# A transformer block on one core: the adapter attention joined to the first maxima in 16 turns, a tail that begins with the third tile's products, and weight splits of 512 columns

## The reference, cut to what matters

```python
mod = (silu(c) @ wmod).reshape(1, 6, 1, C); sa, ca, ga, sb, cb, gb = ...
h = layernorm(x) * (1 + ca) + sa
q, k, v = split(h @ w_attn.T)                 # 32 heads of 32, q and k rotated
y = softmax(causal(q @ k.T / sqrt(32))) @ v
ak, av = split(adapter_wte @ w_attn.T)[1:]    # 10 rows
y = y + gating[0] * softmax(q @ ak.T / sqrt(1024)) @ av
x = x + ga * (y @ w_proj.T)
h = layernorm(x) * (1 + cb) + sb
x = x + gb * top2_mixture_of_experts(h, gate_w, expert_w)
```

## Time and profile before

| | |
|---|---|
| median of 3 runs | 2748.28 us |
| the profiled execution | 2752.79 us, span 2751.0 us |
| granted TensorE clock, mean | 0.948 of full speed |
| busy share | PE 91%, DVE 60%, POOL 48%, ACT 38% |
| `front` | 0 to 680 us |
| `adapter_attention` | 680 to 809 us |
| `attention` up to the main loop's first exponential | 809 to 880 us |
| main loop and first two tiles | 880 to 2010 us |
| `tail`: projections and routing | 2010 to 2290 us |
| `tail`: experts | 2290 to 2751 us |

### The profile page before, as it was taken

The page is one execution under the profiler, slowest core; times in us unless marked ns, Lnnn a source line. Parts: engine busy times, 40 slices in busy tenths (PEclk is TensorE's granted clock), DMA queues, the critical chain, the costliest instruction groups (busy, mean ns, idle before and its releaser), DMA issues. The chain is left out here.

```text
span 2751.0 us, 40043 instructions
## 1 busy us (share of the span) xinstructions
PE 2493.5 (91%) x13407; PEld 1626.6 (59%) x13407; DVE 1657.0 (60%) x3261; ACT 1048.0 (38%) x1877; POOL 1308.5 (48%) x827
## 2 busy tenths in 40 slices
PE   6789999998758999999999999999859875999997
PEld 4667677776534444444444444444348764888885
DVE  5544555110558777777777777777526554777775
ACT  3521011111331555555555555555501111444443
POOL 4452342000432767676767666667724443333232
PEclk9999999999886999999999999999979987999998
DMA  7356655212743515151515151512356754878885
GB/s 262 108 161 192 176 167 169 93 39 63 261 131 78 134 37 134 38 133 40 131 40 132 40 127 40 120 48 55 106 190 214 162 122 175 307 284 292 306 288 179
DMA packets 231903, 397.21 MB, mean 144 GB/s; under 512 B 44540, under 2 KB 95292, under 8 KB 231620
## 3 DMA queue, kind: packets, MB, share of 16 engines
q1 hardware_dynamic: 204340, 319.62, 40.2%
q0 software_dynamic: 17152, 50.38, 5.3%
q10 hardware_dynamic: 10256, 25.21, 2.9%
HBM read 299.22 MB, written 103.76 MB: 146 GB/s over the span
## 5 line engine op out<-in xcount | busy, mean ns | idle before, releaser
L1227 ACT ACTIVATE t_prob<-t_scores_psum 128x512 f32<-128x512 f32 (+3 forms) x1280 | 610.5, 538 | 449.2 <-PE t_scores_psum L1102 242.4
L1355 POOL TENSOR_TENSOR t_two<-t_prob 128x1024 f32<-128x1024 f32 (+1 forms) x321 | 694.4, 2184 | 166.5 <-ACT t_prob L1227 103.2
L1255 DVE TENSOR_REDUCE t_part<-t_seen_psum 128x1 f32<-128x512 f32 x768 | 479.5, 683 | 146.4 <-PE t_seen_psum L1075 142.3
L1075 PE MATMUL t_seen_psum<-t_k_stack,t_q_stack 97*128 97x512 f32 (+3 forms) x1283 | 523.4, 420 | 40.1 <-DVE t_q_stack L1243 22.5
L1098 PE MATMUL t_scores_psum<-t_q_stack,t_k_stack 98*128 98x512 f32 (+3 forms) x1280 | 504.2, 405 | 8.7 <-ACT t_prob L1227 7.4
L1098 PEld LDWEIGHTS t_scores_psum<-t_q_stack,t_k_stack 98*128 98x128 f32 x1280 | 243.0, 191 | 307.8 <-ACT t_prob L1227 172.5
L1075 PEld LDWEIGHTS t_seen_psum<-t_k_stack,t_q_stack 97*128 97x128 f32 x1283 | 257.5, 201 | 92.3 <-DVE t_part L1255 37.1
L1261 DVE CUSTOM_DVE_ANT_0 t_seen_psum<-t_seen_psum,t_causal 128x128 f32<-128x128 f32 (+3 forms) x515 | 250.7, 505 | 100.5 <-PE t_seen_psum L1075 90.2
L1116 PE MATMUL t_y_acc_psum<-t_prob,t_v 128*32 128x512 f32 (+3 forms) x2576 | 302.7, 542 | 0.0
L1630 PE MATMUL acc_psum<-z_e_hi,z_x_hi 128*128 128x512 f32 x576 | 228.4, 397 | 0.0
L1632 PE MATMUL acc_psum<-z_e_hi,z_x_lo 128*128 128x512 f32 x576 | 225.4, 391 | 0.0
(11 more groups left out here) (240 smaller groups left out, 3834.0 us busy)
## 6 DMA issues: line engine op xcount, KB each, us to landing
z_raw<-in_expert_w SPq DMA_DIRECT2D x80, 512.0 KB, 5.7
z_spare<-in_expert_w SPq DMA_DIRECT2D x72, 512.0 KB, 6.0
f_w_raw<-in_wmod SPq DMA_DIRECT2D x8, 2048.0 KB, 10.3
t_q_stack<-scratch_q_hi SPq DMA_DIRECT2D x64, 256.0 KB, 4.9
t_k_stack<-scratch_k_hi SPq DMA_DIRECT2D x64, 256.0 KB, 5.2
f_w_raw<-in_w_attn SPq DMA_DIRECT2D x24, 512.0 KB, 6.1
t_inverse<-scratch_inverse SPq DMA_DIRECT2D x132, 64.0 KB, 2.0
t_y<-scratch_a_y SPq DMA_DIRECT2D x33, 256.0 KB, 4.6
```

The source lines that it names most:

```text
L1075: nc.tensor.matmul(seen[:, n % BANKS, 0:width], q_stack[par][0:SEEN, h, t0:t0 + P], k_stack[par][0:SEEN, h, c * CH:c * CH + width], start= ...
L1227: nc.scalar.activation(prob[:, step % RING, h, c0:CH], scores[:, score_bank(step, h), c0:CH], ACT.Exp, scale=1.0 / math.sqrt(D)).then_inc( ...
L1255: nc.vector.tensor_reduce(dst, seen[:, n % BANKS], AX.X, ALU.max).then_inc(seen_free, 1)
L1355: nc.gpsimd.tensor_tensor(two[:, pair % 2, heads, c0:CH], a, b, ALU.add).then_inc(two_ready, 1)
```

## The change

The separate program for the adapter goes. Its work moves into the head of `attention`, in 16 turns of 1024 tokens of one group, and the 78 first entries of `order` are dealt out over the turns, half a share twice in a turn. `ak` and `av` stay where `front` left them, the buffers of the turns lie in the space of the second stacks and of v. The scores have 40 columns instead of 128 (8 products a turn), the spread of the weights goes from DVE to POOL (now with the inverse alone, the gating being multiplied into `av` once), the four memsets on POOL are put between turns, and the two on DVE go, since the stack of q loses its row of zeros (`see` has 96 rows instead of 97, `score` 97 instead of 98). The weight split begins at step 44, a piece of 512 columns every two steps, the copy on ACT and the difference on DVE. The tail loads ga first, DVE waits for ga alone, and PE's first work is the product of tile 2.

```diff
-def adapter_attention(nc, sem, consts, ak, av, q_hi_d, q_lo_d, out):
...
-        P_FROM, P_EVERY = STEPS - 20, 2
+        P_FROM, P_EVERY = STEPS // 2 + Y_LAG + 2, 2
...
-            c, at = divmod(step - lag - P_FROM, P_EVERY)
-            return c if i == G // 2 - 1 and at == 0 and 0 <= c < KC else None
+            piece, at = divmod(step - lag - P_FROM, P_EVERY)
+            return divmod(piece, 2) if i == G // 2 - 1 and at == 0 and 0 <= piece < 2 * KC else (None, 0)
...
+        def head_share(t, half):
+
+            at = [HEAD * x // (2 * TURNS) for x in (2 * t + half, 2 * t + half + 1)]
+            return range(*at) if t < TURNS else range(0)
...
+            def load_pair(t):
+                g, col = a_group(t)
+                if t >= 2:
+                    sp.wait_ge(a_q_ready, t - 1)
+                for src, dst in zip(q_parts, a_parts):
+                    sp.dma_start(dst[:, t % 2], src[g, :, col]).then_inc(a_loaded_q[t % 2], 16)
...
+            load_pair(0)
+            load_quarter(0)
...
+            for t in range(TURNS):
+                if t + 1 < TURNS:
+                    load_pair(t + 1)
+                if 1 <= t + 1 < NQ:
+                    load_quarter(t + 1)
+                if t == NQ:
+                    sp.dma_start(v[0][:, :, :], v_d[0]).then_inc(first_loaded[NQ], 16)
...
+            def a_score(t):
+
+                g = a_group(t)[0]
+                pe.wait_ge(a_q_ready, t + 1)
+                if t >= 2:
+                    pe.wait_ge(a_shifted, t - 1)
+                for j in range(2 * TPC):
+                    last = nc.tensor.matmul(a_scores(t)[:, j * HG * A:(j + 1) * HG * A], a_q[:, t % 2, j * P:(j + 1) * P],
+                                            ak[:, g].rearrange("p (h a) -> p h a", a=D)[:, :, 0:A], start=True, stop=True)
+                last.then_inc(a_scores_ready, 1)
...
+            def a_multiply(t, x):
+                pe.wait_ge(a_turn_ready, t + 1)
+                if (t, x) == (0, 0):
+                    pe.wait_ge(a_gated, 1)
+                else:
+                    pe.wait_ge(a_y_ready, 2 * t + x)
+                nc.tensor.matmul(y_acc[:, :], av[:, a_group(t)[0]], a_turn[:, t % 2, x * CH:(x + 1) * CH],
+                                 start=True, stop=True).then_inc(a_acc_ready, 1)
...
+            for t in range(TURNS + 2):
+                if t < TURNS:
+                    a_score(t)
+                head(t, 0)
+                if t >= 2:
+                    a_multiply(t - 2, 0)
+                    a_multiply(t - 2, 1)
+                head(t, 1)
+                if 1 <= t <= TURNS:
+                    if t == 1:
+                        pe.wait_ge(consts_loaded, 64)
+                    a_turn_over(t - 1)
...
+            pe.wait_ge(one_rows_set, 2)
             pe.wait_ge(sums_set, 2)
...
+            for t in range(TURNS + 2):
+                if t < TURNS:
+                    a_exp(t)
+                if t >= 2:
+                    a_keep_y(t - 2, 0)
+                    a_keep_y(t - 2, 1)
+                    a_store(t - 2)
+                if 1 <= t <= TURNS:
+                    a_keep_turned(t - 1)
...
+                    c, o = chunk_at(i, step, 3)
+                    if c is not None:
+                        act.wait_ge(p_loaded[c % 2], 16 * (c // 2 + 1))
+                        nc.scalar.activation(half_of(p_hi[:, c], o), half_of(p_raw[c % 2], o), ACT.Copy).then_inc(p_hi_done, 1)
...
-            for n in range(HEAD):
-                advance(0, n)
...
+            for t in range(TURNS):
+                if t > 0:
+                    dve.wait_ge(a_shifted, t)
+                a_shift(t)
+                head(t, 0)
+                if t > 0:
+                    dve.wait_ge(a_inv_ready, t)
+                a_norm(t)
+                head(t, 1)
...
-                        nc.vector.tensor_copy(p_hi[:, c], p_raw[c % 2]).then_inc(p_hi_done, 1)
-                        dve.wait_ge(p_hi_done, c + 1)
-                        nc.vector.tensor_tensor(p_lo[:, c], p_raw[c % 2], p_hi[:, c], ALU.subtract).then_inc(p_lo_done, 1)
+                        dve.wait_ge(p_hi_done, 2 * c + o + 1)
+                        nc.vector.tensor_tensor(half_of(p_lo[:, c], o), half_of(p_raw[c % 2], o), half_of(p_hi[:, c], o), ALU.subtract).then_inc(p_lo_done, 1)
...
+            for t in range(TURNS):
+                a_spread(t)
+                if t + 2 < TURNS:
+                    a_add(t + 2)
+                if t == 4:
+                    one_row(0, t)
+                if t == 7:
+                    nc.gpsimd.memset(prob[:, :, :, :], 1.0).then_inc(sums_set, 1)
+                if t == 10:
+                    nc.gpsimd.memset(two[:, :, :, :], 1.0).then_inc(sums_set, 1)
+            pool.wait_ge(a_scores_ready, TURNS)
+            one_row(1, TURNS - 1)
...
-        CONSTS = 16 * 8
+        CONSTS = 16 * 7
...
+            load_row(ga, 2, ga_loaded)
             load_y(EARLY)
             load_x(0)
+            load_row(scale_b, 4, consts_loaded)
+            load_row(shift_b, 3, consts_loaded)
             load_y(EARLY + 1)
...
             for n in range(EARLY, NT + LAG):
+                if n == EARLY:
+                    project(n)
                 if n == LAG:
                     pe.wait_ge(consts_loaded, CONSTS)
                     pe.wait_ge(made, 1)
                 if n >= LAG:
                     turn(n - LAG)
-                if n < NT:
+                if EARLY < n < NT:
                     project(n)
...
-            dve.wait_ge(consts_loaded, CONSTS)
+            dve.wait_ge(ga_loaded, 16)
```

More of the change, by code:

```diff
@@ L840, in attention @@
         p_hi, p_lo = p_parts
+        with ExitStack() as inner:
+            ab = lambda name, shape: inner.enter_context(nc.sbuf_tensor(f"a_{name}", shape, F32))
+            ab("filler", [P, 2 * HG * T])
+            a_y, a_turn = ab("y", [P, 2, 2 * CH]), ab("turn", [P, 2, 2 * CH])
+            a_prob, a_weight = ab("prob", [P, 2, 2 * CH]), ab("weight", [P, 2, AM, A])
+            a_top, a_total, a_inv = ab("top", [P, AM]), ab("total", [P, AM]), ab("inv", [P, 2, AM])
+            a_q, a_parts = ab("q", [P, 2, 2 * CH]), [ab(f"q_{n}", [P, 2, 2 * CH]) for n in ("hi", "lo")]
         q_stack, k_stack = [None, None], [None, None]
@@ L1031, in fetch @@
                 par, g = (1, ds(i * 2 + 1)) if half == 0 else (0, ds((i * 2 + 2) % G))
+                if (i, half, c, part) == (0, 0, 0, 0):
+                    for b in range(2):
+                        sp.wait_ge(a_stored[b], 16 * (TURNS // 2))
+                    sp.wait_ge(a_acc_ready, 2 * TURNS)
                 if (c, part) == (0, 0):
@@ new lines, in head @@
+            def head(t, half):
+                for n in head_share(t, half):
+                    if order[n][0] == "see" and order[n][3:] == (0, 0, 0):
+                        pe.wait_ge(first_loaded[order[n][2]], LOADS - 16)
+                    advance(0, n)
+            for t in range(TURNS + 2):
[8 more added lines that the diff above has]
+                    if t == 1:
+                        pe.wait_ge(consts_loaded, 64)
+                    a_turn_over(t - 1)
```

301 lines of the change are left out of this document (117 added, 184 removed).

## The result

The changed kernel takes 2727.61 us (median of 5, 2724.83 to 2730.89) beside 2751.15 us of before; the ratio is 0.990, 95% interval 0.9883 to 0.9916. It is faster by some 24 us, where I had forecast 67. The sign was right; the size was not, and 2727.6 lies above the range that I gave (2655 to 2720).

| part | marks in the traces | before | after | measured | forecast |
|---|---|---|---|---|---|
| A, joint stage | main loop's first exponential | 879.5 | 851.9 | −27.7 | −51 |
| main loop | from there to the 28th store of y's high part | 944.0 | 943.1 | −0.9 | 0 |
| B, weight split | 28th to 33rd (last) of these stores | 175.2 | 190.4 | +15.2 | −3 |
| C, tail | last store to the end | 752.3 | 740.3 | −12.0 | −13 |

What follows compares the result with a forecast made beforehand. PE was taken to bound nearly everything, except around 780 us and at the tail's start. From the median 2748.3 us, −51 −3 −13 = −67 gave 2681 us, own range 2660 to 2700, stated range 2655 to 2720.

Steps and rivals of the forecast that it cites:

- A: Joint stage of adapter and head: main loop's first exponential at 828.4 us, −51 us (−40 to −62).
- B: Weight split: copies go to ACT, half of the differences to steps 48 to 63; −3 us (−7 to +3).
- C: Tail: ga loads first and tile 2's product fills PE's wait; −13 us (−8 to −18).
- What bounds the kernel: PE nearly everywhere, except around 780 us and the tail's start; DMA, memsets and DVE pace stretches before the main loop.
- a turn at 6.6 us: Joint stage: PE's work and waits for 1024 tokens sum to 6.7, rounded to 6.6 us (6.2 to 7.6).
- the hand-off: Within a joint-stage turn: the second `av` product waits for ACT's copy of the shared PSUM tile, about 0.8 us.
- ten further turns at 6.6: Joint stage: after turn 5 at 744 us, ten turns bring the last scores to 810 us.
- the start: Joint stage's first turns: scores stand behind loads, coming near 690, 701, 712, 724 and 737 us, turn 5 at 744.
- memsets absorbed: Joint stage: slack of 3.2 us and a turn of lag absorb POOL's 6.92 us memsets, within a few us.
- The clock rival: Joint stage: PE's clock stays at its lower level, 12.9 us a turn, first exponential +17, total 2749 us; chance 0.10.
- The DMA rival: Joint stage: DMA bounds all of it, 157 us, first exponential at 858, total 2711 us; chance 0.09.
- No overlap: Joint stage: turns do not overlap, 16 us each, first exponential at 949, total 2802 us; chance 0.04.

Runs made afterwards that it cites:

- e7: The kernel of e2 with the second product of a turn in another bank than the first; 2695.8 us, ratio to before 0.981.
- e2: The changed kernel with the head's two rows of negative maxima issued by SP behind all loads of the turns; 2700.9 us, ratio to before 0.982.
- e12: The changed kernel with the split's 16 differences replaced by one-input multiplications by 1.0 on DVE; 2725.3 us, ratio to before 0.989.
- The seven traces: Traces of the changed kernel and six follow-up runs with the same joint stage; first exponentials between 846.9 and 864.7 us.
- e8: The kernel of e2 with the loads of the first group's quarters spread over the turns; 2691.3 us, ratio to before 0.980.
- e5: The changed kernel with the early weight split in pieces of 1024 columns every four steps, 8 differences instead of 16; 2717.7 us, ratio to before 0.988.
- e6: The changed kernel with the split's 512-column pieces one in each step from the last 20 steps on; 2717.6 us, ratio to before 0.987.
- e1: The changed kernel with the weight split as it was before the change; 2711.2 us, ratio to before 0.986.

## Why the prediction was wrong, step by step

- **What bounds the kernel**: right. PE's holes were where the page had them, and they were what could be gained. (Of slices 11 to 13 I wrote "5 and 9"; they read 7, 5 and 8. The 46.8 us are all of DVE's work, not its plain reductions alone. Neither enters the sum.)
- **A, where it went**: the first exponential came 23.5 us later than the forecast 828.4. The start has 7.6 of them (turn 5 at 751.6 instead of 744), the ten further turns 15.0 (81.0 instead of 66), the end 0.9.
- **A, a turn at 6.6 us**: right for an undisturbed turn, 6.2 to 6.7, with the hand-off at 0.8 to 0.9; e7 takes it away and has turns of 5.5. Scores 1.9, products 1.0 each, turned blocks 1.0. The last memset was covered by the last products, and the end took 19.3 us, as in the sum (18 to 19).
- **A, "ten further turns at 6.6"**: the step that failed, by omission. I listed what each moved step puts on PE, DVE, ACT and POOL and wrote that PE takes its entries in order, but not that SP does too: `load_row` waits for `minus_ready`, and the next turns' q stand behind it. SP stood still for 32.3 us in two waits. e2 moves only these rows: its ten turns take 66.6 us, and the first exponential goes from 851.9 to 834.2. A hole also costs more than its wait, since the turns behind it run at the lower clock: of the ten turns four took 9.6 us or more in the changed kernel, six in e12 and none in e2.
- **A, the start**: mechanism right, size too small. Turn 1 came at 706.2, not 701, and turn 5 at 751.6, not 744. The rate was the one in my sum (1 MB and 1.57 MB in 3.2 and 8 us are some 230 GB/s, measured 228). SP issued q of turn 1 only at 694.2, behind a quarter and the constants; the sum has no term for the constants, but no run parts what they cost. The seven traces have turn 5 at 746.1 to 754.1. e8 shows that most of this start was not needed.
- **A, memsets absorbed**: true only while POOL has its lead. Behind a late add the 6.92 us of one memset reached PE (1.71 and 1.21 us, and the lower clock for a turn and a half). In e2 the add for turn 6 starts 5.5 us ahead of that turn's scores, here 2.7; there the same memset costs PE 0.34 us.
- **B**: sign wrong, +15 in this trace. Over five traces with the changed split the stretch is 186.2 us in the mean, over five with the old split 176.5: about 10, outside my −7 to +3. I priced only what the sums of POOL lose and put the price of the early differences at nothing, since PE would have "about 1 us of slack a step". The slack was about right (behind blocks of 2.94 and 2.40 us PE waited 1.71 and 1.48), but it can't take such blocks. What the earlier trace rows showed, 3.28 against 1.23, was not a slower DVE but a wait for POOL's instruction and the work behind it: two pieces of the kernel before end 1.09 and 1.08 us behind a pair sum. Sixteen pieces can wait more often than eight; that this is what costs isn't shown (e5), that the place costs is (e6). The gain that I had counted didn't come either: PE waited 1.9 us for a pair sum in this stretch before and after.
- **C**: right, −12 (forecast −13; alone −14, 9 to 20). `gate(1)` came 44.7 us behind the boundary, forecast 43.
- **The clock rival** (0.10): false over the stage, with a mean of 0.91 from 750 to 852 us, and 1.00 from 785 to 803, though turned blocks were part of each turn. Behind the holes it was true for a while: the turn behind the first takes 10.8 us at a clock of 0.50, where I had 12.9 for that level; in e1 two turns behind the second hole take 11.9 and 11.7 us, with 0.50 from 805 to 829. It was true for the five first turns too, where PE mostly waited. **The DMA rival** (0.09) held for the same five turns and in the changed kernel for no more (0.50 of the engines' time from 750 to 852). **No overlap** (0.04): false.

Together: A −28 for −51, B +15 for −3, C −12 for −13. A and B lie outside the ranges that I gave them. The −28 is one trace; the seven of that stage give −24 in the mean.

## What to carry to other kernels

An instruction that waits holds back everything behind it in its own queue, SP's too: when loads with different deadlines and one semaphore wait share a queue, put the wait behind all loads that don't need it. When DVE gets a two-input instruction beside POOL, price it by what is left of POOL's instruction plus its own work, and put it where nobody needs DVE within that time. Loads that are merged into a busy start should be ordered by when they are first used, not by when they were issued before.
